# The first weight product of a logic-tower kernel over the whole batch by pairs of k tiles, wider idle products, and a later second setup

## The reference

```python
e = jnp.stack([tbl_0[ids[:, 0]], ..., tbl_7[ids[:, 7]]], axis=1)        # 512 x 8 x 1024
x_not = jnp.take(e, not_idx, axis=1)
t = jnp.tanh(jax.nn.relu(x_not @ Wn1 + bn1) @ Wn2 + bn2)
iv = e.at[:, not_idx, :].set(t)
# pair_fuse: relu(concat(iv[p0], iv[p1]) @ W1 + b1) @ W2 + b2, for two and-pairs and one or-pair
z = (and_out.sum(1) + or_out.sum(1) + rest) / count
h = jnp.maximum(jnp.concatenate([z, dense_ctx], 1) @ W_top1 + b_top1, 0.0)
y = jnp.maximum(h @ W_top2 + b_top2, 0.0) @ W_top3
```

## Time and profile before

| | |
|---|---|
| median of three runs | 545.06 us (544.74 to 545.12) |
| the profiled execution: span from first to last instruction | 553.3 us |
| PE busy | 533.0 us, 96% of the span |
| DVE / ACT / POOL busy | 357.8 / 248.1 / 234.2 us |
| the chain that ended last, by engine | PE 81%, DVE 6%, POOL 4% |
| mean granted PE clock | 0.991 |

### The profile page before, as it was taken

How to read it: one execution, slowest core, us unless ns; L and a number is a source line. 1 busy time by engine, 2 the same in 40 slices (tenths; PEclk the granted TensorE clock), 3 DMA queues, 4 the chain that set the end, 5 groups by cost and what they waited for, 6 DMA issues and landing times.

```text
span 553.3 us, 6173 instructions
## 1 busy us (share of the span) xinstructions
PE 533.0 (96%) x2392; PEld 441.2 (80%) x2392; DVE 357.8 (65%) x370; ACT 248.1 (45%) x301; POOL 234.2 (42%) x176
## 2 busy tenths in 40 slices
PE   5799969899899999999999999999999999999998
PEld 5698848778688888888888788888888888888885
DVE  5367899799766686788746688852423784345832
ACT  3375277365456634444444645331335432142343
POOL 5408888569817636022077107855545400000000
PEclk9799989999999999999999999999999999999999
DMA  7917866582596576369089435999999983331000
GB/s 254 330 44 175 160 168 201 167 178 89 125 213 184 145 105 181 94 95 153 18 170 300 160 103 154 267 248 247 247 246 248 247 247 105 97 108 39 0 1 0
DMA packets 38607, 87.31 MB, mean 158 GB/s; under 512 B 4305, under 2 KB 4561, under 8 KB 38578
## 3 DMA queue, kind: packets, MB, share of 16 engines
q0 software_dynamic: 18624, 49.29, 41.2%
q1 hardware_dynamic: 19522, 37.51, 21.3%
q10 hardware_dynamic: 432, 0.11, 0.1%
HBM read 86.90 MB, written 0.00 MB: 157 GB/s over the span
## 4 chain that ended last, share of the span: by engine, by line
PE 81%; DVE 6%; POOL 4%; DMA 2%; issue 2%; ACT 2%; another core or an unknown queue 1%; DVEq 0%; ACTq 0%
PE PS L1063 78%; POOL XR L483 4%; DMA XR<-table,rows 2%; DVE XR L890 2%; DVE WO L797 1%; PE PS L1092 1%; ACT WO L591 1%; PE PS L1241 1%; DVE XR L965 1%; DVE XR L942 1%; PE PS L1213 1%; DVEq L389 0%; DVE XO L873 0%; DMA XR<-ints 0%
## 5 line engine op out<-in xcount | busy, mean ns | idle before, releaser
L1063 PE MATMUL PS<-XO,WO 128*128 128x512 f32 (+1 forms) x2256 | 510.5, 388 | 11.6 <-DVE WO L797 8.7
L1063 PEld LDWEIGHTS PS<-XO,WO 128*128 128x128 f32 x2256 | 420.3, 190 | 99.8 <-DVE WO L797 11.5
L591 ACT ACTIVATE WO<-WR 128x1024 fp32r<-128x1024 f32 x93 | 98.6, 1060 | 240.1 <-PE PS L1063 220.8
L797 DVE TENSOR_TENSOR WO<-WR,WO 128x1024 fp32r<-128x1024 f32 x93 | 113.7, 1222 | 141.4 <-ACT WO L591 126.2
L483 POOL DMA_INDIRECT XR<-table,rows x96 | 127.5, 1328 | 60.0 <-issue 28.3
L621 ACT ACTIVATE XO<-XR 128x1024 fp32r<-128x1024 f32 (+1 forms) x76 | 79.3, 1046 | 9.9 <-DVE XR L942 7.9
L505 POOL DMA_DIRECT2D WR<-weights x30 | 37.4, 1657 | 98.6 <-DVE WO L797 54.1
L873 DVE TENSOR_TENSOR XO<-XR,XO 128x1024 fp32r<-128x1024 f32 x60 | 73.0, 1217 | 1.0 <-ACT XO L621 0.5
L568 POOL DMA_INDIRECT XR<-table,rows_rest x32 | 55.5, 1735 | 39.0 <-DMA XR<-table,rows_rest 36.6
L890 DVE STREAM_TRANSPOSE XR<-XR 128x1024 f32<-128x1024 f32 x26 | 55.7, 2149 | 3.5 <-DMA XR<-table,rows 3.5
L942 DVE TENSOR_TENSOR XR<-XR 128x1024 f32<-128x1024 f32 (+1 forms) x32 | 38.6, 1219 | 0.0
(11 more groups left out here) (72 smaller groups left out, 117.5 us busy)
## 6 DMA issues: line engine op xcount, KB each, us to landing
WR<-weights SPq DMA_DIRECT2D x71, 512.0 KB
WR<-weights POOLq DMA_DIRECT2D x30, 512.0 KB, 7.4
XR<-table,rows POOLq DMA_INDIRECT x110
XR<-table,rows_rest POOLq DMA_INDIRECT x32, 12.7
XR<-dense_t SPq DMA_DIRECT2D x3, 32.0 KB, 3.1
XR<-w_dense SPq DMA_DIRECT2D x3, 32.0 KB, 3.0
XR<-ints SPq DMA_DIRECT2D x1, 84.0 KB, 2.1
XR<-identity ACTq DMA_DIRECT2D x1, 64.0 KB, 2.9
```

Of the source, the lines that this page charges most:

```text
L591: nc.scalar.activation(WO[:, n % 2, 0, :], WR[:, slot, :], ACT.Copy).then_inc(w_hi, 1)
L797: V_.tensor_tensor(WO[:, n % 2, 1, :], WR[:, raw_slot(n), :], WO[:, n % 2, 0, :].bitcast(FP32), ALU.subtract).then_inc(w_lo, 1)
L1063: mm = nc.tensor.matmul(PS[:, bank, cols], WO_t[:, slot, ws, i, k, :], XO[:, x0 + k, xs, cols], start=first and k == 0 and n == 0, stop=la ...
```

## The change

1. The idle products have 512 columns, not 128 (the identity is read four times over), and there are 10, 6 and 3 of them: at the start, after the first two tiles' turns, after the next two tiles' turns. Before there were 18, and three times 2.
2. Entry 0 runs over the whole batch in two steps of a pair of k tiles: first the k tiles 0 and 1 for the four output tiles (24 products of 512 columns), then, after 16 transposes for the k tiles 4 to 7, the k tiles 2 and 3 (24 products), with the 16 transposes of field 1 ahead of the last 6. The first product now waits for all four tiles of field 0. Each half batch and pair has its bank (`2 * h + pair % 2`), and ACT and DVE take the pairs in this new order.
3. DVE's two sums of weights (L816) come after all eight low parts of field 0.
4. `setup_rest` moves from t = 12 to t = 44, the register reads from t = 24 to t = 50. The scratch that it needs lies in a tensor of its own (`small`, 384 numbers a partition), so POOL's wait for `setup_done` moves from ahead of the gathers of field 4 to ahead of the gathers of the remaining fields at the end.

```diff
-IDLE_PRODUCTS = 18
+IDLE_PRODUCTS = (10, 6, 3)
+def x1_done(pair):
+    return pair + 1
 def x0_done(h, pair):
-    return 4 * h + pair + 1
+    return 4 * (pair // 2) + 2 * h + pair % 2 + 1
+SETUP_AT, REGS_AT = 44, 50
+        small = sb("small", [P, 384], FP32)
...
             gather_half(3, 1)
-            pool.wait_ge(setup_done, 1)
             gather_half(4, 0)
...
+            pool.wait_ge(setup_done, 1)
             pool.wait_ge(x_lo, x_done(entry_of(2, Q3, 1), 1))
...
+            for low in (0, 2):
+                for h in range(2):
+                    x0_hi(h, low)
+                    x0_hi(h, low + 1)
+                for h in range(2):
+                    x0_keep(h, low)
+                    x0_keep(h, low + 1)
...
+            for low in (0, 2):
+                for h in range(2):
+                    x0_lo(h, low)
+                    x0_lo(h, low + 1)
+            for i in range(2):
+                dve.wait_ge(raw_in[2 + i], 16)
+                V_.tensor_tensor(WR[:, i, :], WR[:, i, :], WR[:, 2 + i, :], ALU.add).then_inc(t1_sum, 1)
...
-                    if t == 12:
+                    if t == SETUP_AT:
                         setup_rest()
-                    if t == 24:
+                    if t == REGS_AT:
...
-                    nc.tensor.matmul(PS[:, KT - 1, 0:P], ident[:, :], ident[:, :], start=True, stop=True)
+                    nc.tensor.matmul(PS[:, KT - 1, :], ident[:, :], ident[:, :].unsqueeze(1).broadcast_to([P, 4, P]),
+                                     start=True, stop=True)
...
+            def turn_first_field(h, pair):
+                if pair > 1:
+                    pe.wait_ge(x0_raw, x0_done(h, pair - 2))
+                for k in range(2 * pair, 2 * pair + 2):
+                    for b in range(2 * h, 2 * h + 2):
+                        turn = turn_rows(flat(ROW_BUF), b, k, 2 * h + pair % 2)
+                turn.then_inc(x0_turned, 1)
+
+            keep_running(IDLE_PRODUCTS[0])
+            for h in range(2):
+                for b in range(2 * h, 2 * h + 2):
+                    pe.wait_ge(x0_in[b], 16)
+                turn_first_field(h, 0)
+                turn_first_field(h, 1)
+                keep_running(IDLE_PRODUCTS[1 + h])
...
                 if e == 0:
-                    for i in range(2):
+                    for kk in range(2):
+                        pe.wait_ge(x_lo, x0_done(1, kk))
                         for m in range(4):
-                            mm = product(bank0 + m, m // 2, m % 2, x0, i == 0, True,
-                                         x0_there if m == 0 else None, half_batch(i))
-                            if i == 1:
+                            mm = product(bank0 + m, m // 2, m % 2, x0, kk == 0, kk == 1, ks=range(2 * kk, 2 * kk + 2))
+                            if kk:
                                 mm.then_inc(quarter, 1)
+                            if (kk, m) == (0, 3):
+                                for h in range(2):
+                                    turn_first_field(h, 2)
+                                    turn_first_field(h, 3)
+                            elif (kk, m) == (1, 2):
+                                turn_second_field()
```

More of the change, by code:

```diff
@@ L252, in flat, with keep @@
             return XR[:, buf, :, :].rearrange("p k b -> p (k b)")
-        setup_f = flat(SETUP_BUF)
-        at = [0]
+        early, kept_f = flat(SETUP_BUF), small[:, :]
+        at = {"early": 0, "kept": 0}
         def scratch(n):
-            at[0] += n
-            return setup_f[:, at[0] - n:at[0]]
+            at["early"] += n
+            return early[:, at["early"] - n:at["early"]]
+        def keep(n):
+            at["kept"] += n
+            return kept_f[:, at["kept"] - n:at["kept"]]
         int_in = scratch(INTS).bitcast(INT32)
-        cst = scratch(CONSTS)
         ident_in = scratch(P)
         row4 = scratch(GROUPS * F)
-        row_t = scratch(BT * F)
-        prod_t = scratch(2 * BT * F)
         rows_f = scratch((SLOTS - 1) * GROUPS)
         rows0_f = scratch(2 * BT)
[L269 to L278, removed]
-        prods = scratch((SLOTS - 1) * GROUPS * F)
+        prods = scratch((SLOTS - 1) * GROUPS * F)
+        cst = keep(CONSTS)
+        row_t = keep(BT * F)
+        prod_t = keep(2 * BT * F)
+        hot = keep(SLOTS * F)
+        in_pair, rest, is_not, wx, tmp8 = (keep(F) for _ in range(5))
+        both = keep(2 * PAIR_SLOTS * F)
+        sel = keep(2 * PAIR_SLOTS)
+        buf_f = keep(PAIR_SLOTS)
+        buf_d = keep(PAIR_SLOTS)
+        wt_prod = keep(2 * F)
+        wt = keep(2)
+        same = keep(1)
+        cnt = keep(1)
         def rest_tile(b):
@@ L1057, in _, with product @@
         def _(pe):
-            def product(bank, slot, i, x0, first, last, before_k=None, cols=slice(0, B)):
-                for k in range(4):
+            def product(bank, slot, i, x0, first, last, before_k=None, ks=range(4)):
+                for k in ks:
                     if before_k is not None:
@@ L1062, in product @@
                     for n, (ws, xs) in enumerate(((0, 0), (0, 1), (1, 0))):
[L1063 to L1064 removed]
+                        mm = nc.tensor.matmul(PS[:, bank, :], WO_t[:, slot, ws, i, k, :], XO[:, x0 + k, xs, :],
+                                              start=first and k == ks[0] and n == 0, stop=last and k == ks[-1] and n == 2,
                                               skip_group_check=True)
@@ L1136, in _, with turn_second_field @@
+            def turn_second_field():
+                for b in range(2):
+                    pe.wait_ge(x1_in[b], 16)
+                for pair in range(4):
+                    pe.wait_ge(x0_raw, x0_done(pair // 2, 2 + pair % 2))
+                    for k in range(2 * pair, 2 * pair + 2):
+                        for b in range(2):
+                            turn = turn_rows(staging(1, 0), b, k, pair)
+                    turn.then_inc(x1_turned, 1)
             for e in range(OZ):
```

99 lines of the change are left out of this document (16 added, 83 removed).

## The result

The changed kernel is slower: 547.45 us (median of six runs, 545.43 to 549.92) against 545.09 us (six runs of the kernel before on the same chip, 544.74 to 546.54), a ratio of 1.0048 with a 95% interval of 1.0026 to 1.0069. I had forecast 542.7 us, with 537.0 to 546.8 as the range.

What follows compares the result with a forecast made beforehand. PE, busy 96% of the 553.3 us span, bounds the kernel; gains must come before 151.67 us. t = 28 starts 10.9 us earlier, 0.3 us is added back: 553.3 - 10.6 = 542.7 us, range 537.0 to 546.8.

Steps and rivals of the forecast that it cites:

- the stall and the lower clock behind it: PE's slow issue at 19.5 to 24.06 us and 1.2 GHz at 22 to 29; 7.0 us, absent from timed runs.
- (d): PE's wait of 2.35 us ahead of 111.37 us (t = 28); 1.2 us of it taken as absent from timed runs.
- rival A: PE's stall at 19 to 24 us is in every run, so the whole 10.6 us counts: 534.5 us; chance 0.12.
- The 8.2 us: Excess of the profiled span, 553.3 us, over the median time, 545.06; taken as losses the timed runs lack, and added back.
- Idle products: Ten products of 512 columns at the start: over by 9.8 us, no cost; the next six cost 0 to 1.4.
- The first product: PE's first product at 17.0 us (16.4 to 17.8), before 14.56; entry 1 at 31.5, a 1.4 us undisturbed loss.
- rival C: Clock: PE at lower level for first products (3.5 us), or behind 16 transposes (4.1 more): 544.5 to 546.8 us; chance 0.14.
- Transposes and their waits: In entry 0, the 16 for k tiles 4 to 7 and 16 of field 1 wait for nothing, about 1 us spare.
- The setup at t = 12: Taking DVE's setup away there gains 4.75 us net (3.0 to 5.5); PE then waits 1.3 us at t = 18.
- Field 3's gathers: POOL's last rows for t = 25 land about 96.5 us; PE starts t = 28 at 100.5, waiting 1.8 us.
- rival B: POOL's gathers, finding fewer DVE gaps between t = 4 and t = 28, take the whole gain: 546.8 us; chance 0.13.
- The setup at t = 44, the registers at t = 50: Near t = 48 PE waits 0.2 us (0 to 1.5); registers' gain at t = 24 hidden; 0.3 us cost booked.

Runs made afterwards that it cites:

- parts 1 to 3 alone: The changed kernel with the second setup back at t = 12 and the registers at t = 24: 547.86 us, ratio 1.0035 to the kernel before.
- part 4 and the early gathers: Kernel before with second setup at t = 44, registers at t = 50, and field 2's first eight gathers ahead of POOL's wait: 538.92 us, ratio 0.9884.
- group 1: First of three groups on two other chips: kernel before 554.71 us, changed kernel 548.06, part 4 and the early gathers 561.46.

## Why the prediction was wrong, point by point

- **What bounds the kernel.** Right on the first chips: entry 0 ends at 30.1 us undisturbed, as worked out, and the stall and the lower clock behind it are not there; nor is the wait (d) at t = 28. On the two others rival A's premise probably holds (the times of the kernel before fit a stall in every run), and the change then wins 7 us at most by the medians, not its 10.6 us.
- **The 8.2 us.** A term of the sum that was mis-sized. It is the difference of a span and a time, and 553.3 - 10.6 is a span too. The two spans of the kernel before differ by 10.0, and 545.06 - 10.6 + 10.0 gives 544.5 us in place of 542.7. So 1.8 of the 4.75 us by which the forecast was short are arithmetic, and 2.9 are left for the mechanism.
- **Idle products.** Right: over at 9.9 us (forecast 9.8), no cost.
- **The first product.** A term of the sum that was mis-sized. I had 17.0 us (16.4 to 17.8); it was 18.12 in the profile, and 16.27 to 17.84 in others (19.19 in one with the stall just ahead of it). The last tile of field 0 was there at 16.0 and not at 14.3: POOL's third gather took 1.93 us in place of 0.94, beside DVE's first weight splits. The kernel before has the same long third gather and does not feel it, since its first product needs two tiles only. The first product then ran at half clock for 3.4 us (+1.2): the first half of rival C. Entry 1 came at 33.8 us, not 31.5; over the experiments, the one with that stall aside, it was 30.8 to 33.8, and the new first product cost 2.2 us in time (parts 1 to 3 alone) where I had 1.4.
- **Transposes and their waits.** Right: the 16 of the k tiles 4 to 7 and the 16 of field 1 wait for nothing. They stay at the upper clock, so the second half of rival C did not come. By the rule weighed in the prediction ("TensorE: Matmul & The Clock Gate", Part 4, in the Trainium skill), they might have cost it; this trace shows no such cost, with two stretches of 1.7 us at 1.00.
- **The setup at t = 12.** Right up to t = 18: no wait at t = 16, one of 1.62 us at t = 18 (forecast 1.3), 4.6 us won there (forecast 4.75).
- **Field 3's gathers.** This is the step that failed. I wrote that POOL's queue "runs without a pause since t = 4 and moves only with the start", and so kept each gather's duration. But the durations change with what DVE does beside them. With the setup gone, the queue lost 5.1 us between its 12th and 24th gather, DVE waited 3.54 us for rows already in the turn at t = 17, and nothing of the 4.75 us was left. Those rows are field 2's, for which the sum had no term at all; the wait of 1.8 us that I had at t = 28 did not come, and that quarter started at 105.5 us (82.23 and 96 products, with 1.3 us for the lower clock) in place of 100.5. That is the mechanism of rival B, to which I gave 0.13, though it too looked at field 3; its price for the whole kernel, 546.8 us, was near the 547.45 measured, in part by luck, since it starts from 1.4 us for the first product. I had even its condition (a slack "now negative") in hand and priced it from one gather only.
- **The setup at t = 44, the registers at t = 50.** Right: hidden. Setup ran from 155.2 to 159.5 us, and PE has no wait there (booked 0.3).

The section on two separate sides of "SBUF — State Buffer" in the Trainium skill is the rule that would have spoken for rival B: VectorE and GpSimd share ports. The held gathers here last until about 1 us after DVE's run of instructions with two operands in SBUF ends (65.11 to 69.67 us), which fits it; but other gathers beside the same run took 0.95 and 1.97 us, so the trace bears the rule out only in part.

## What to carry to other kernels

A gain on the engine that everyone waits for is real only up to the next queue: when DVE work is taken out ahead of a wait, ask how far ahead the queue of the DMA-issuing engine is of each instruction that waits for it, and give its durations a range that covers its longest ones, since they change with the pattern beside them. Two moves that are each worth nothing can be worth 1.2% together (part 4 and the early gathers), so a move that shows no gain is to be tried again once its follower is out of the way. And a kernel that wins on one chip is to be timed on another: the order of the kernels here was turned round by a stall that no line of their code explains.

## What the hardware showed that I had not expected

- An indirect gather of 128 rows takes POOL 0.95 us and 0.30 to the next, or much more beside some runs of DVE instructions: 4.56 and 4.45 us in the changed kernel's profile, 11.60 in the earlier trace rows, and 14.12 at most, in part 4 with early gathers of group 1. In the changed kernel the gathers of 4.56, 4.45 and 9.52 us each ended 0.8 to 1.0 us after DVE came to a transpose or to a pause.
- 4.75 us more work for DVE made a kernel about 3 us faster.
- A stall of PE's issue (15 instructions in 14 us instead of 94), seen in eight of the nine profiles on the last two chips and in one earlier profile, the first of the kernel before. The times of the kernel before fit it in all 42 runs there, and in none of 57 on the first chips (none above 548.2 us).
